# QKV products in halves of 288 columns, and three reorderings, in a windowed attention and convolution kernel on one core

## What is computed

```
x = x + L0(_gn(x))      # attention in windows of 8x8 pixels
x = x + L1(_gn(x))      # x + its Laplacian, then a 1x1 product

# L0, for each window of N = 64 tokens, 6 heads of 32 channels:
qkv = x @ [QK_w; V_w].T + bias                      # 192 -> 576 channels
o = irfft2(rfft2(q * SCALE) * rfft2(k))             # over the window's 8x8
attn = softmax(einsum("nd,md->nm", o, v) + position_bias)
y = attn @ v
return y @ proj_w.T + proj_b
# L1:
out = x + conv3x3(x, laplacian)                     # per channel
return conv1x1(out, merge_w) + merge_b
# _gn: mean and variance over 6 channels x 128 x 128, 32 groups an image
```

## Time and profile before

| | |
|---|---|
| median of 3 runs | 6497.19 us (6494.64 to 6500.95) |
| profiled execution | 6496.43 us, its span 6494.6 us |
| PE busy | 6218.2 us, 96% of the span |
| DVE busy | 5311.9 us, 82% |
| ACT busy | 3663.8 us, 56% |
| POOL busy | 2065.2 us, 32% |
| chain that ended last | PE 57%, DVE 24%, POOL 10%, ACT 7% |
| granted TensorE clock, mean | 0.992 |

### The profile page before, as it was taken

How to read it: one execution, slowest core, us unless ns; L and a number is a source line. 1 busy time by engine, 2 the same in 40 slices (tenths; PEclk the granted TensorE clock), 3 DMA queues, 4 the chain that set the end, 5 groups by cost and what they waited for, 6 DMA issues and landing times.

```text
span 6494.6 us, 222120 instructions
## 1 busy us (share of the span) xinstructions
PE 6218.2 (96%) x95620; PEld 5308.6 (82%) x95620; DVE 5311.9 (82%) x11941; ACT 3663.8 (56%) x9024; POOL 2065.2 (32%) x2310
## 2 busy tenths in 40 slices
PE   7999999999999999999999999999999999999987
PEld 5888788888888888888888888888888888888875
DVE  5777788888888888888888888888888888888878
ACT  3666655555555555555555555555555555555540
POOL 1333333333333333333333333333333333333320
PEclk9999999999999999999999999999999999999999
DMA  3211223223323222322332322332333332232226
GB/s 130 67 61 42 62 75 105 85 65 104 91 85 96 75 83 85 109 75 80 92 96 85 93 77 84 92 104 65 89 94 91 89 81 64 65 86 65 69 73 166
DMA packets 378996, 551.42 MB, mean 85 GB/s; under 512 B 23399, under 2 KB 283562, under 8 KB 365739
## 3 DMA queue, kind: packets, MB, share of 16 engines
q1 hardware_dynamic: 378028, 537.21, 28.7%
HBM read 335.80 MB, written 201.33 MB: 83 GB/s over the span
## 4 chain that ended last, share of the span: by engine, by line
PE 57%; DVE 24%; POOL 10%; ACT 7%; issue 2%; SPq 0%; DMA 0%; DVEq 0%; ACTq 0%
PE b_q L467 13%; PE b_t L516 7%; POOL probs L959 6%; PE b_s L536 5%; PE b_s L429 4%; DVE qkl L812 4%; DVE bn L717 4%; PE b_o L506 4%; ACT probs L916 3%; DVE late L820 3%; DVE ssum L830 3%; PE b_s L496 3%; DVE smax L729 3%; POOL xl L954 3%; ACT qkh L871 3%; PE b_o L405 2%
## 5 line engine op out<-in xcount | busy, mean ns | idle before, releaser
L948 POOL TENSOR_TENSOR probs<-probs,srec 128x384 f32<-128x384 f32 x1024 | 849.3, 829 | 3709.1 <-DVE srec L863 3709.1
L812 DVE TENSOR_TENSOR qkl<-b_q,qkh 128x384 fp32r<-128x384 f32 x1024 | 569.5, 556 | 615.7 <-ACT qkh L871 604.0
L959 POOL TENSOR_TENSOR probs<-probs,smax 128x384 f32<-128x384 f32 x1024 | 907.7, 886 | 415.1 <-DVE smax L729 415.1
L724 DVE TENSOR_TENSOR probs<-b_s,posb 128x384 f32<-128x384 f32 x1024 | 553.3, 540 | 331.6 <-PE b_s L536 330.7
L916 ACT ACTIVATE probs<-probs 128x384 f32<-128x384 f32 x1024 | 535.5, 523 | 481.0 <-POOL probs L959 480.3
L467 PE MATMUL b_q<-wnh,xh 128*128 128x192 f32 (+1 forms) x2048 | 790.7, 386 | 3.2 <-DVE xhl L834 2.7
L871 ACT ACTIVATE probsT<-b_s 128x384 f32<-128x384 f32 x1024 | 502.8, 491 | 503.2 <-PE b_s L429 503.2
L871 ACT ACTIVATE qh<-b_t 94x384 f32<-94x384 f32 x1024 | 497.8, 486 | 465.5 <-PE b_t L516 465.5
L536 PEld LDWEIGHTS b_s<-vT,osb 32*64 32x64 f32 x24576 | 450.2, 132 | 286.1 <-ACT osb L871 205.5
L871 ACT ACTIVATE yT<-b_s 128x256 f32<-128x256 f32 x1024 | 392.7, 384 | 460.7 <-PE b_s L496 459.1
L820 DVE SCALAR_TENSOR_TENSOR late<-b_s,pb,xs 128x128 f32<-128x128 f32 (+1 forms) x2048 | 610.5, 340 | 27.5 <-PE b_s L486 5.7
(11 more groups left out here) (154 smaller groups left out, 15129.2 us busy)
## 6 DMA issues: line engine op xcount, KB each, us to landing
ld<-in_x SPq DMA_DIRECT2D x96, 1024.0 KB, 4.9
late<-x_dram SPq DMA_DIRECT2D x112, 640.0 KB, 6.2
xs<-in_x SPq DMA_DIRECT2D x128, 512.0 KB, 5.6
x_dram<-late SPq DMA_DIRECT2D x128, 512.0 KB, 2.8
out<-late SPq DMA_DIRECT2D x128, 512.0 KB, 4.6
late<-x_dram SPq DMA_DIRECT2D x240, 192.0 KB, 6.6
xs<-in_x SPq DMA_DIRECT2D x128, 256.0 KB, 6.2
x_dram<-late SPq DMA_DIRECT2D x128, 256.0 KB, 3.6
```

Of the source, the lines that this page charges most:

```text
L812: V.tensor_tensor(qkl[:, :], q_out, qkh[:, :].bitcast(F32), ALU.subtract).then_inc(lo_out, 1)
L948: P.tensor_tensor(probs[:, i % 3, :, :], probs[:, i % 3, :, :], srec[:, i % 2, :].unsqueeze(2).broadcast_to([128, 6, N]), ALU.mult).then_i ...
L959: P.tensor_tensor(probs[:, i % 3, :, :], probs[:, i % 3, :, :], smax[:, i % 2, :].unsqueeze(2).broadcast_to([128, 6, N]), ALU.subtract).th ...
```

## The change

Four parts, in the words of the diff:

1. QKV. The 576 columns are two halves of 288: columns 288 to 575 (the last 96 of k, and v), then 0 to 287. `b_q` holds them back to back around the boundary of its two banks, from column 224 on. The transposed v moves from `b_q` to the free ends of `b_t`'s two banks. With that PE's wait for `vT_out` of the pair before goes, and two new ones come: `prod_done` of the pair before ahead of the transposes of v, and `vT_out` ahead of L516.
2. POOL does L959 before the `xl` of the same iteration, not after.
3. `group_mean`, `group_spread` and the two bias parts of image 0 are issued among the 64 position steps, ahead of steps 8, 16, 40 and 52.
4. From `ALONE` on, the residual x1 of pieces 0 to 3 is added by one more product with the identity on PE, and ACT instead of DVE reads their result (`a_read` is its semaphore).

```
-        q_out, v_psum, vt_out = b_q[:, 0:QK], b_q[:, 512:512 + C], b_q[:, 512 + C:512 + C + 256]
+        first = 512 - QKV // 2
+        q_out, v_psum = b_q[:, first:first + QK], b_q[:, first + QK:first + QKV]
+        vt_out = b_t.rearrange("p (t c) -> p t c", t=2)[:, :, QK:512]
...
             for m in range(N):
+                if m == 8:
+                    group_mean(0)
+                elif m == 16:
+                    group_spread(0)
+                elif m == 40:
+                    bias(0, 0)
+                elif m == 52:
+                    pe.wait_ge(m_read, 3)
+                    bias(0, 1)
...
-                    mm(o, mats(par, 3 + p // 2), zb[:, k, at:at + 256], start=False, stop=True).then_inc(m_mm, 1)
+                    last = mm(o, mats(par, 3 + p // 2), zb[:, k, at:at + 256], start=False, stop=not alone)
+                    if alone:
+                        last = mm(o.rearrange("p (r c) -> p r c", c=W), ident[:, :],
+                                  src_a[v % 3][:, 2 * p + 1:2 * p + 3, 1:W + 1], start=False, stop=True)
+                    last.then_inc(m_mm, 1)
...
-            group_mean(0)
-            group_spread(0)
-            for part in range(2):
-                pe.wait_ge(m_read, 2 + part)
-                bias(0, part)
...
-                    if pair(1):
-                        pe.wait_ge(vT_out, n - 1)
...
-                    for o, lo, up, done in ((v_psum, QK, QKV, v_mm), (q_out, 0, QK, qkv_mm)):
+                    for lo, up, done in ((QKV // 2, QKV, v_mm), (0, QKV // 2, qkv_mm)):
+                        o = b_q[:, first + lo:first + up]
...
                     pe.wait_ge(v_out, n)
+                    if pair(1):
+                        pe.wait_ge(prod_done, n - 1)
...
                     pe.wait_ge(lo_out, n)
+                    pe.wait_ge(vT_out, n)
...
+                        if it < ALONE or p >= 4:
+                            dve.wait_ge(m_mm, m_count[it])
+                            result(at, p, it)
...
+                    act.wait_ge(m_mm, m_count[it])
+                    A.activation(res_a[:, v % 2, p * 256:(p + 1) * 256], m_region(it)[:, 0:256], ACT.Identity,
+                                 bias=mc[:, v // NS % 2, 0:1]).then_inc(a_read, 1)
...
-                h = (it + 4) // 4
-                if it % 4 == 2 and 0 <= h < PAIRS // 4:
-                    pool.wait_ge(xh_done, 3 * h + 2)
-                    P.tensor_tensor(tokens(xl, 0, h), windows(0, h), tokens(xh, 0, h).bitcast(F32), ALU.subtract
-                                    ).then_inc(xl_done, 1)
                 if pair(2):
                     i, n = pair(2)
                     pool.wait_ge(max_done, n)
...
+                h = (it + 4) // 4
+                if it % 4 == 2 and 0 <= h < PAIRS // 4:
+                    pool.wait_ge(xh_done, 3 * h + 2)
+                    P.tensor_tensor(tokens(xl, 0, h), windows(0, h), tokens(xh, 0, h).bitcast(F32), ALU.subtract
+                                    ).then_inc(xl_done, 1)
```

More of the change, by code:

```diff
@@ L222, in program, with m_wait @@
         iterations = range(-4, 8 * BLOCKS)
-        m_count, used = {-5: 4}, 4
+        ALONE = PAIRS + 2 * 8
+        m_count, d_count, a_count = {-5: 4}, {-5: 4}, {-5: 0}
         for it in iterations:
-            used += m_task(it) is not None
-            m_count[it] = used
-        ALONE = PAIRS + 2 * 8
+            by_act = it >= ALONE and it % 8 < 4
+            m_count[it] = m_count[it - 1] + (m_task(it) is not None)
+            d_count[it] = d_count[it - 1] + (m_task(it) is not None and not by_act)
+            a_count[it] = a_count[it - 1] + (m_task(it) is not None and by_act)
         def m_region(it):
             return b_q[:, 0:256] if it >= ALONE and it % 2 else b_o[:, 192:512]
-        def m_free(it):
-            return m_count[it - 2] if it > ALONE else m_count[it - 1]
+        def m_wait(eng, it):
+            eng.wait_ge(m_read, d_count[it])
+            if a_count[it]:
+                eng.wait_ge(a_read, a_count[it])
         def pairs():
@@ L354, in _, with group_mean, group_spread, bias @@
             pe.wait_ge(hid_relu, 2 * (N * N // 512))
-            for m in range(N):
+            m_out = m_region(0)
+            def group_mean(b):
+                pe.wait_ge(g1_aggr, b + 1)
+                mm(m_out[:, 0:1], part_mates[:, :], gst[:, 0:1], start=True, stop=True).then_inc(m_mm, 1)
+            def group_spread(b):
+                pe.wait_ge(g1_dev, b + 1)
+                if b == 0:
+                    pe.wait_ge(m_read, 1)
+                mm(m_out[:, 0:2], part_spread[:, 0:CA], gst[:, 0:2], start=True, stop=True)
+                mm(m_out[:, 2:4], part_spread[:, CA:256], gst[:, 0:2], start=True, stop=True).then_inc(m_mm, 1)
+            def bias(b, part):
+                pe.wait_ge(norm0_w, b + 1)
+                lo, up = part * QKV // 2, (part + 1) * QKV // 2
+                o = m_out[:, 0:QKV // 2]
+                mm(o, ones[0:1, :], qkvb[:, lo:up], start=True, stop=False)
+                mm(o, negmean[:, 0, :], wn[:, 0, lo:up], start=False, stop=False)
+                mm(o, negmean[0:CB, 1, :], wn[0:CB, 1, lo:up], start=False, stop=True).then_inc(m_mm, 1)
+            for m in range(N):
+                if m == 8:
[7 more added lines that the diff above has]
+                    bias(0, 1)
                 for t in range(2):
@@ L365, in _ @@
             last.then_inc(pos_mm, 1)
-            m_out = m_region(0)
-            def group_mean(b):
-                pe.wait_ge(g1_aggr, b + 1)
-                mm(m_out[:, 0:1], part_mates[:, :], gst[:, 0:1], start=True, stop=True).then_inc(m_mm, 1)
[L373 to L378, removed]
-                pe.wait_ge(norm0_w, b + 1)
-                lo, up = part * QKV // 2, (part + 1) * QKV // 2
-                o = m_out[:, 0:QKV // 2]
-                mm(o, ones[0:1, :], qkvb[:, lo:up], start=True, stop=False)
-                mm(o, negmean[:, 0, :], wn[:, 0, lo:up], start=False, stop=False)
-                mm(o, negmean[0:CB, 1, :], wn[0:CB, 1, lo:up], start=False, stop=True).then_inc(m_mm, 1)
             def channels(field, width):
@@ L401, in piece @@
                 par, k, o = v // NS % 2, v % 2, m_region(it)[:, 0:256]
+                alone = it >= ALONE
                 if p == 0:
@@ L435, in _ @@
                     kind, at, p = task
-                    pe.wait_ge(m_read, m_free(it))
+                    m_wait(pe, it - 2 if it > ALONE else it - 1)
                     if kind == "piece":
@@ L469, in _ @@
                     pe.wait_ge(v_out, n)
+                    if pair(1):
+                        pe.wait_ge(prod_done, n - 1)
                     for t in range(2):
-                        last = nc.tensor.transpose(vt_out[:, t * 128:(t + 1) * 128],
+                        last = nc.tensor.transpose(vt_out[:, t, :],
                                                    vs[:, i % 5, t * N:t * N + 128], ident[:, :])
@@ L705, in result @@
                 par = v // NS % 2
-                if p == 0 and v >= 2:
+                if (p == 0 or (p == 4 and it >= ALONE)) and v >= 2:
                     dve.wait_ge(out_sent[v % 2], 48 * (v // 2))
@@ L893, in _ @@
                     sqrt(sm[:, 6, :], sm[:, 4, :])
+                task = m_task(it)
+                if it >= ALONE and task and task[0] == "piece" and task[2] < 4:
+                    _, v, p = task
+                    if p == 0:
+                        act.wait_ge(out_sent[v % 2], 48 * (v // 2))
+                    act.wait_ge(m_mm, m_count[it])
+                    A.activation(res_a[:, v % 2, p * 256:(p + 1) * 256], m_region(it)[:, 0:256], ACT.Identity,
+                                 bias=mc[:, v // NS % 2, 0:1]).then_inc(a_read, 1)
                 if pair(4):
@@ L921, in _ @@
                     act.wait_ge(vT_mm, n)
-                    copy(vT[:, i % 2, :, :].rearrange("p t m -> p (t m)"), vt_out).then_inc(vT_out, 1)
+                    copy(vT[:, i % 2, :, :], vt_out).then_inc(vT_out, 1)
                 if pair(4):
```

10 lines of the change are left out of this document (4 added, 6 removed).

## The result

The changed kernel takes **6466.16 us** (6465.26 to 6466.6, 5 runs), the kernel before 6497.58 beside it (6494.64 to 6500.95, 5 runs): ratio 0.995, 95% interval 0.9936 to 0.9965. That is 31 us less where the forecast was 79 less. The profiled execution took 6465.69, its span is 6463.9 (before 6494.6).

A forecast was written before the change was run, and what follows sets the result against it. PE's steps bound phases 1 to 5, a ring through DVE, POOL and ACT phases 6 to 0. Terms -58 + 14 + 4 - 21 - 17 - 10.5 + 9 = -79.5 gave 6418 us, range 6360 to 6474.

The forecast's parts named there:

- POOL's order: Subtraction ahead of `xl`: phase 6 gains 0.23 us, -21 us over 86 blocks; phase 2 loses nothing; first image -17 us.
- QKV in halves: PE's QKV products: 288-column steps of 0.132 us save 0.11 us a pair in phases 1 to 5, -58 us.
- The straight line: Rival on QKV products: a 288-column step takes 0.143 us, the halves give nothing, 6476 us; chance 0.13.
- 288 as 384: Rival on QKV products: 288 columns cost as much as 384, 159 us worse instead of 58 better, 6635 us; chance 0.06.
- the late copy of v: Rival on ACT's copy of v: 0.15 us spare is too little, each PE-paced pair loses 0.06, 6450 us; chance 0.14.
- The forecast's limit for "slower": QKV products: from a 288-column step of 0.158 us on, the halves cost what the rest of the change gives.
- The wait for `prod`: PE ahead of the transposes of v: 0.13 us in 104 phases 0, +14 us; +4 us in the first image.
- the ring: DVE, POOL and ACT set the pace from phase 6's scores to phase 0's `qkl`, covering phase 7's wait for `prod`.
- POOL goes first: Rival in phase 6: L959 holds the ports because it starts first, 55 us more gain, 6363 us; chance 0.13.
- The first image: No stencil there: POOL's order gains 17 us in phases 6, 2 and 0; the wait for `prod` costs 4.
- The opening: Image 0's statistics and bias parts among the position steps: L834 starts at 86.5 and not 97.39, -10.5 us.
- The tail: From `ALONE` on: DVE's result of piece 4 waits for PE, block cycle 10.25 us instead of 9.68, +9 us.

The follow-up runs named there:

- e2: The changed kernel with `xl` again ahead of POOL's subtraction in phase 2 alone, from iteration 136 on: 6418.64 us.
- e8: The changed kernel with DVE's second diagonal operation of a strip (L688) moved from phase 2 to phase 3, POOL's new order kept: 6420.4 us.
- e5: The changed kernel with the QKV columns split as before, 192 and 384, all else as changed: 6518.34 us.
- e4: The changed kernel with PE's transposes of v behind the projection's four products instead of ahead of them: 6429.88 us.
- e1: The changed kernel with POOL's old order everywhere, `xl` ahead of the subtraction in phases 2 and 6: 6456.73 us.
- e9: The changed kernel; in phase 6 DVE's stencil operation waits for POOL's subtraction, and `xl` waits for that stencil operation: 6397.45 us.
- e11: The changed kernel with a DVE write of zeros to 96 scratch columns between `prod` and the stencil operation in phase 6: 6464.19 us.
- e12: The changed kernel with a DVE write of zeros to 288 scratch columns between `prod` and the stencil operation in phase 6: 6492.9 us.
- e13: The changed kernel with a DVE reduction over 128 columns of a constant tile between `prod` and the stencil operation in phase 6: 6406.48 us.
- e3: The changed kernel with the tail as before: DVE reads all six pieces and adds the residual, PE has no identity product: 6458.99 us.

## Why the forecast was off

**The step that failed** is the last of "POOL's order": in phase 2 `xl` "comes after it beside the stencil. At worst it holds DVE for 0.25 (L686 takes 0.93 in rows 4 against 0.68)", and `qkl` has 0.7 to spare. L686 in the earlier trace rows was held by only the last part of an `xl` that had begun long before. No row gave a reason why an `xl` that is released in the middle of two such operations should cost the later one less than its whole length. It cost L688 1.08 (1.90 - 0.82) and phase 2 0.35 us of period beside the 0.1 that the halves gave: 48 us by e2, 46 by e8. I had costed POOL's operation in its old place and asked of the new place only how long `xl` can wait, not whom it can hold. With 48 added, the -79 of the sum is the -31 that was measured; the other terms were off by up to 9 us each, and that these cancel is luck.

**QKV in halves: right.** Forecast -58 in five phases with a step of 0.132; measured 0.132, and 52 us in four phases with the split undone (e5). With phase 2 free (e2) the fifth has its 0.10 too (5.84 for 5.94), some 11 us more. The straight line (0.143), 288 as 384 (0.173) and the late copy of v (no wait at L488 in the PE-paced phases) fall. The forecast's limit for "slower", a step of 0.158, was wrongly worked out: ten steps instead of five of 0.1125 and five of 0.173, in 530 pairs, cost the 21.5 us that the rest gives from a step of 0.147 on.

The Trainium skill's "TensorE: Matmul & The Clock Gate", section "Back-to-back issue gap", would give 0.1225 for 288 columns by its formula for isolated products; the measured 0.132 is 0.01 longer, as it was with 384 columns.

**The wait for `prod`: the right cause, mis-sized.** From `prod`'s end at 4057.18 L488 came 0.14 later and L534 another 2.09, so 2.23 where the forecast had 2.16: 0.20 an occurrence and not 0.13. Each block pays it once, which is 21 us by e4 and not 14. The growth stands in phase 7's period, where L488 waits as well (from `prod`'s end at 1.58 after the first QKV product, L534 at 3.81 for 3.61). But DVE's `prod` of phase 0 did not come later for it: it ends 1.72 after a first QKV product that is itself 0.20 later, where before it ended 1.92 after it. So phase 7's wait is covered by the ring, as forecast, and it is phase 0's that costs. In the first image phases 0 and 4 grew by 0.20 each, 32 x 0.20 = 6 and not 4.

**POOL's order in phase 6: right.** 1.67 with a lead of 0.30, as the earlier trace rows had it, and a period 0.24 shorter (forecast 0.24); e1 against e2 has 23 us for it in iterations 144 to 1023 (forecast 21). "POOL goes first" falls for this place, and e9 prices it: 69 us beyond what the new order gave (the rival had 55).

The Trainium skill's "SBUF — State Buffer", section "Who interferes with whom", has the engine that issues first hold the ports and the other fully block. Full blocking agrees nearly: a held subtraction ends 0.68 to 0.69 after DVE's last holding operation in phase 6 of after, e11 and e12, where alone it takes 0.83, and a held `xl` 1.13, where alone it takes 1.27. Issue order as the start times of the rows show it doesn't, as 0.30 and 0.39 of lead weren't enough; 0.37 and 0.45 were in other places. On Trainium2 this section of the Trainium skill counts only operations with two SBUF inputs and the faster modes as such that hold; e12 beside e13 shows that writing zeros does.

**The first image** gave 12.3 us in iterations 0 to 127; forecast -17 + 4 = -13. Phases 2 and 6 gained 0.26 and 0.72 as forecast, and phase 7 0.13. Phase 0 lost 0.20, where I had 0.19 gained less 0.13.

**The opening: right.** The first QKV product comes at 87.71 and not at 98.23, 10.5 earlier, and `xhl` starts at 86.88 (forecast 86.5).

**The tail: right in its cycle, off in its clock.** 10.44 for 10.25: piece 4's result starts 6.75 after PE's start (forecast 6.73), and what DVE does behind it takes 3.69 for 3.5. The forecast of +9 is near the 7 of e3. That the old tail has more blocks at half clock than the new one, I hadn't weighed.

**The sum again with what was measured**: halves -63 (five phases), the wait +21 + 6, POOL's order -23 in phase 6 (e1 against e2) and -17 in the first image, opening -10.5, tail +7 and 5 more for the longer half-clock stretch, and the step that was missed, +48: -26.5, against -30.7 of the two spans; 4 us stay unassigned. One step was put at nothing; the others held to 9 us each.

## What to carry to other kernels

When an operation on GpSimd moves, list the VectorE operations with two SBUF inputs (and writes of constants) around its **new** place, and charge the one behind it with nearly GpSimd's whole duration (here 1.08 of 1.27), unless GpSimd's lead over the first of them is as long as the 0.5 to 0.6 us that sufficed here. A new wait of PE delays all that is queued behind it: put what doesn't need the awaited thing ahead (e4: 36 us). Where GpSimd is on the critical path, it can pay to put a one-input operation of VectorE between the release and the next two-input one, even a useless one (0.28 us a block for 60 us here), or to let the two-input one wait for GpSimd (69 us).

## What was not expected of the hardware

- Writing zeros with VectorE takes part in holding GpSimd (1.71 with 96 columns, 1.92 with 288), a reduction as long as the 288 zeros doesn't (0.83).
- GpSimd, once held by one operation of VectorE, gets through before the next in after's phase 2 (`xl` 1.72, then L688 1.90). Yet in five iterations of before it was held through four instructions in a row, 2.78 us. The rows (`x2` is two instructions):

```profile
4005.94 2.78 POOL L959 TENSOR_TENSOR probs<-probs,smax 128x384 f32<-128x384 f32 x1
4005.95 0.68 DVE L686 SCALAR_TENSOR_TENSOR late<-late 128x512 f32<-128x512 f32 x1
4006.55 0.82 DVE L670 TENSOR_TENSOR dg<-late 128x645 f32<-128x645 f32 x1
...
4007.29 0.74 DVE L806 TENSOR_SCALAR mn<-wm,sm 128x384 f32<-128x384 f32 x2
```

  L959 ends at 4008.72, 0.69 after L806's end, so that this operation with one SBUF input held it too. One thing differs in the rows: in phase 2 of after `xl` starts 0.10 after L704 had begun and goes next, 110 of 110 times; here L959 starts 0.01 before L686. In iterations 138 and 140 of after, too, the subtraction starts 0.30 before L704, and it is passed by L688 as well (2.74 and 2.41 us). That a place in the queue depends on this fits these rows; no run tested it.
